# Causal mask of the row maxima: from a TensorE matmul to the VectorE instruction that takes the maximum

## The reference

```python
def attn(x, wq, wk, wv, wo):                  # x: 2 x 2048 x 1024, 32 heads of 32, one shared k and v
    q = (x @ wq).reshape(B, T, N_HEADS, HEAD_DIM)
    k = x @ wk
    v = x @ wv
    scores = jnp.einsum('bqhd,bkd->bhqk', q, k) * scale
    scores = jnp.where(causal[None, None], scores, -jnp.inf)
    probs = jax.nn.softmax(scores.astype(jnp.float32), axis=-1)
    out = jnp.einsum('bhqk,bkd->bqhd', probs, v).reshape(B, T, C)
    return out @ wo
def ffn(x, A, B, Wr, br):                     # 8 LoRA experts of rank 16, softmax router
    scores = H * jax.nn.softmax(jnp.einsum('bsd,hd->bsh', x, Wr) + br, axis=-1)
    low = jnp.einsum('bsd,hrd->bshr', x, A)
    return SCALING * jnp.einsum('bshr,hor,bsh->bso', low, B, scores)
x = x + layernorm(attn(layernorm(x)))
x = x + layernorm(ffn(layernorm(x)))
```

## Time and profile before

| what | value |
|---|---|
| time, 3 executions | median 3809.69 us (3802.37 to 3811.74) |
| the profiled execution: its own time | 3814.41 us |
| its span, first to last instruction | 3812.6 us |
| granted TensorE clock, mean | 0.953 of full speed |
| busy: PE, VectorE, ScalarE, GpSimd | 3486.0, 2466.2, 1574.0, 1927.6 us |
| diagonal head slots, mask matmuls L981 | 1024, 1024 |

### The profile page before, as it was taken

How to read it: one execution, slowest core, us unless ns; L and a number is a source line. 1 busy time by engine, 2 the same in 40 slices (tenths; PEclk the granted TensorE clock), 3 DMA queues, 4 the chain that set the end, 5 groups by cost and what they waited for, 6 DMA issues and landing times.

```text
span 3812.6 us, 47714 instructions
## 1 busy us (share of the span) xinstructions
PE 3486.0 (91%) x17496; PEld 1691.6 (44%) x17496; DVE 2466.2 (65%) x5584; ACT 1574.0 (41%) x3089; POOL 1927.6 (51%) x510
## 2 busy tenths in 40 slices
PE   5889999999999999899988999999999999999984
PEld 3444444444444444444444444444444444444432
DVE  3556776766767677874366667676777766667434
ACT  0223344444455444445322334344444554445541
POOL 0224455645455756566521355566355656566750
PEclk8989998999999999999998899999999999999995
DMA  3312111111011000001111211111100110000000
GB/s 79 121 42 76 33 38 34 56 34 37 20 34 56 20 26 26 20 20 29 62 51 38 71 34 45 32 40 51 39 26 26 29 30 24 26 20 15 18 1 33
DMA packets 132330, 144.19 MB, mean 38 GB/s; under 512 B 28024, under 2 KB 93560, under 8 KB 132096
## 3 DMA queue, kind: packets, MB, share of 16 engines
q1 hardware_dynamic: 132096, 141.13, 12.6%
HBM read 72.91 MB, written 16.78 MB: 24 GB/s over the span
## 4 chain that ended last, share of the span: by engine, by line
PE 69%; DVE 14%; POOL 7%; ACT 4%; issue 3%; SPq 2%; DMA 1%; POOLq 0%; ACTq 0%; DVEq 0%
PE ps L992 12%; PE ps L964 11%; PE ps L1007 11%; PE ps L978 11%; PE ps L1103 9%; POOL ds L514 5%; DVE mx L720 4%; DVE xr L818 2%; PE ps L1144 2%; PE ps L1016 2%; PE ps L1059 2%; SPq L415 2%; POOL ds L511 2%; PE ps L1038 2%; PE ps L1132 1%
## 5 line engine op out<-in xcount | busy, mean ns | idle before, releaser
L720 DVE TENSOR_REDUCE mx<-ps 128x1 f32<-128x512 f32 (+3 forms) x2560 | 1482.5, 601 | 939.2 <-PE ps L981 496.2
L555 ACT ACTIVATE pr<-ps 128x512 f32<-128x512 f32 (+3 forms) x2560 | 1321.8, 535 | 1651.5 <-PE ps L995 858.1
L514 POOL TENSOR_TENSOR ds<-ds,pr 128x2048 f32<-128x2048 f32 (+3 forms) x384 | 1565.2, 4076 | 572.3 <-ACT pr L555 546.2
L992 PE MATMUL ps<-qs,ks 98*128 98x512 f32 (+3 forms) x2560 | 1399.7, 550 | 53.8 <-ACT pr L555 38.6
L978 PE MATMUL ps<-ks,qs 96*128 96x512 f32 (+3 forms) x2560 | 1020.6, 408 | 83.8 <-DVE mx L720 60.7
L992 PEld LDWEIGHTS ps<-qs,ks 98*128 98x128 f32 x2560 | 499.6, 195 | 680.0 <-ACT pr L555 389.5
L511 POOL TENSOR_TENSOR ds<-pr 128x2048 f32<-128x2048 f32 (+1 forms) x64 | 273.3, 4271 | 880.5 <-ACT pr L555 880.5
L1007 PE MATMUL ps<-pr,vs 128*32 128x512 f32 (+3 forms) x5120 | 618.3, 555 | 0.0
L978 PEld LDWEIGHTS ps<-ks,qs 96*128 96x128 f32 x2560 | 510.8, 201 | 226.9 <-DVE mx L720 119.7
L964 PE MATMUL ps<-xT,wq_sb 128*128 128x512 f32 x1024 | 527.9, 616 | 7.3 <-DVE ks L786 4.2
L1103 PE MATMUL ps<-wo_sb,ao 128*128 128x512 f32 x928 | 489.1, 626 | 6.9 <-DVE q L715 2.8
(11 more groups left out here) (123 smaller groups left out, 2011.4 us busy)
## 6 DMA issues: line engine op xcount, KB each, us to landing
qs<-q SPq DMA_DIRECT2D x768, 64.0 KB, 2.0
wq_sb<-in_L_attn_wq_dram SPq DMA_DIRECT2D x64, 512.0 KB, 3.9
t<-in_L_attn_x_dram SPq DMA_DIRECT2D x32, 512.0 KB, 6.4
xr<-in_L_attn_x_dram SPq DMA_DIRECT2D x32, 512.0 KB, 3.5
out_dram<-xr SPq DMA_DIRECT2D x32, 512.0 KB, 2.6
qs<-mT SPq DMA_DIRECT2D x256, 4.0 KB
wo_sb<-in_L_attn_wo_dram SPq DMA_DIRECT2D x1, 4096.0 KB, 13.6
zs<-in_L_ffn_A_dram SPq DMA_DIRECT2D x1, 512.0 KB
```

Source lines behind the costliest of these rows:

```text
L514: nc.gpsimd.tensor_tensor(ds[:, :, c0:], ds[:, :, c0:], this, ALU.add).then_inc(added, 1)
L555: nc.scalar.activation(pr[:, k % NS, g, c0:], ps[:, PST + head(n, t, g) % NPS, c0:], ACT.Exp, scale=SCALE).then_inc(exp_done, 1)
L720: nc.vector.tensor_reduce(mx[:, qt * GH + g, c_:c_ + 1], ps[:, PM + head(n, s, g) % NPM, 0:w], AX.X, ALU.max).then_inc(mx_done, 1)
L992: last = nc.tensor.matmul(ps[:, bank, c0:], ks[0:STK + 2, c:c + P], qs[0:STK + 2, n % NS, g, c0:], start=True, stop=not diagonal)
```

## The change

In `max_scores` the mask matmul L981 is left out. In `maximum` a diagonal head slot is no longer reduced by `tensor_reduce` but by `tensor_tensor_reduce`, which adds `mask_qk` to the bank, writes the sum back to the bank and takes the maximum of it. `mask_qk` becomes 512 columns wide: 384 columns of zeros and then the 128 of the mask, so that its last `w` columns fit a slot of width `w`. In `scores` the mask matmul stays, with `mask_qk` as weights and the identity as the moving operand; `mask_kq` is dropped. The constants that nothing reads (`eps_sb`, `scratch`) are dropped too, and three [128, 1] buffers of the router share one.

```diff
-        mask_qk = sb("mask_qk", [P, P], BF16)
-        mask_kq = sb("mask_kq", [P, P], BF16)
+        mask_qk = sb("mask_qk", [P, BLK], BF16)
...
-        POOL_CONST = 10
+        POOL_CONST = 7
...
-            step(nc.gpsimd.affine_select(out=mask_qk[:, :], in_=mask_qk[:, :], compare_op=ALU.is_ge, fill=NEG,
+            step(nc.gpsimd.affine_select(out=mask_qk[:, BLK - P:], in_=mask_qk[:, BLK - P:], compare_op=ALU.is_ge, fill=NEG,
                                          base=0, pattern=[[-1, P]], channel_multiplier=1))
-            step(nc.gpsimd.memset(mask_kq[:, :], 0.0))
-            step(nc.gpsimd.affine_select(out=mask_kq[:, :], in_=mask_kq[:, :], compare_op=ALU.is_ge, fill=NEG,
-                                         base=0, pattern=[[1, P]], channel_multiplier=-1))
             step(nc.gpsimd.memset(ones[:, :], 1.0))
-            step(nc.gpsimd.memset(eps_sb[:, :], EPS))
...
             def maximum(n, s, g):
-                c_, qt, w, _ = item(n, s)
+                c_, qt, w, diagonal = item(n, s)
+                k = head(n, s, g)
+                seen, found = ps[:, PM + k % NPM, 0:w], mx[:, qt * GH + g, c_:c_ + 1]
                 dve.wait_ge(mx_ready, head(n, s, g) + 1)
-                nc.vector.tensor_reduce(mx[:, qt * GH + g, c_:c_ + 1], ps[:, PM + head(n, s, g) % NPM, 0:w], AX.X,
-                                        ALU.max).then_inc(mx_done, 1)
+                if diagonal:
+                    nc.vector.tensor_tensor_reduce(out=seen, in0=seen, in1=mask_qk[:, BLK - w:], op0=ALU.add, op1=ALU.max,
+                                                   scale=1.0, scalar=3.0 * NEG, accum_out=found).then_inc(mx_done, 1)
+                else:
+                    nc.vector.tensor_reduce(found, seen, AX.X, ALU.max).then_inc(mx_done, 1)
...
-                last = nc.tensor.matmul(ps[:, bank, 0:w], qs[0:STK, n % NS, g, qt * P:(qt + 1) * P],
-                                        ks[0:STK, c:c + w], start=True, stop=not diagonal)
-                if diagonal:
-                    last = nc.tensor.matmul(ps[:, bank, w - P:w], identb[:, :], mask_qk[:, :], start=False, stop=True)
-                last.then_inc(mx_ready, 1)
+                nc.tensor.matmul(ps[:, bank, 0:w], qs[0:STK, n % NS, g, qt * P:(qt + 1) * P],
+                                 ks[0:STK, c:c + w], start=True, stop=True).then_inc(mx_ready, 1)
...
-                    last = nc.tensor.matmul(ps[:, bank, c0:c0 + P], identb[:, :], mask_kq[:, :], start=False, stop=True)
+                    last = nc.tensor.matmul(ps[:, bank, c0:c0 + P], mask_qk[:, BLK - P:], identb[:, :], start=False, stop=True)
```

More of the change, by code:

```diff
@@ L233, in bass_mqa_sandwich_lora_router @@
         identb = sb("identb", [P, P], BF16)
-        mask_qk = sb("mask_qk", [P, P], BF16)
-        mask_kq = sb("mask_kq", [P, P], BF16)
+        mask_qk = sb("mask_qk", [P, BLK], BF16)
         ones = sb("ones", [P, HD])
-        eps_sb = sb("eps_sb", [P, 1])
         xr = sb("xr", [P, 2, D])
@@ L256, in bass_mqa_sandwich_lora_router @@
         ao = sb("ao", [P, NAO, BLK])
-        scratch = sb("scratch", [P, 4])
         m1 = sb("m1", [P, TB])
@@ L261, in bass_mqa_sandwich_lora_router @@
         lg = sb("lg", [P, NF])
-        nlm = sb("nlm", [P, 1])
         le = sb("le", [P, NF])
-        ls = sb("ls", [P, 1])
-        lr = sb("lr", [P, 1])
+        sm = sb("sm", [P, 3])
+        nlm, ls, lr = (sm[:, i:i + 1] for i in range(3))
         lw = sb("lw", [P, NF])
@@ L968, in max_scores @@
             def max_scores(n, s, g):
-                c, qt, w, diagonal = item(n, s)
+                c, qt, w, _ = item(n, s)
                 k = head(n, s, g)
```

## The result

| | before | with the change |
|---|---|---|
| median, 7 executions each | 3809.69 us | 3784.56 us (3774.95 to 3794.28) |
| ratio to before, 95% interval | | 0.9937 (0.9922 to 0.9952) |
| the same, measured again later (g0 below), 11 and 6 executions | 3814.56 us | 3781.52 us; 0.9918 (0.9904 to 0.9933) |
| mean granted clock of the profiled execution | 0.953 | 0.948 |

The account below looks back on a forecast made before the run. PE was taken to set the pace for two thirds of the time (69% of the chain). 54 - 18 + 0.5 = 36.5 us less, 3809.7 - 36.5 = 3773 us; range of 8 in 10 from 3730 to 3815.

Parts of the forecast that it names:

- TensorE gives back 54 us: First term: dropping the mask matmuls in the first pass saves TensorE 54 us, 49 + 12 - 7.
- The bounds of 30 and 87: TensorE's saving: 30 us if followers gain nothing and narrow slots half, 87 if all 1024 masks counted at 0.085.
- 165 narrow slots: Slots of 128 columns where the weight load partly fills the mask's place: 0.04 us off each, 7 us.
- VectorE's slots cost 18 us: Second term: diagonal slots take VectorE 0.156 us more each; 18 us are lost over 18 tight stretches.
- takes a full 0.144 us: VectorE's second instruction, writing one column of `mx`, waits for the first and costs 0.144 us; ends 0.06 and 0.18.
- The rule for idle time: Half of VectorE's idle time in a stretch hides its added 2.5 us; only the rest is lost.
- Small edits, 0.5 us: Fewer constants steps on GpSimd at the start save 0.5 us; exchanged mask operands and shared router buffers give nothing.
- VectorE takes it all back: Rival: VectorE's diagonal slots cost 0.25 us more each, 57 us in all; no change, about 3810 us; chance 0.13.
- Half speed: Rival: VectorE's new instruction needs a second cycle per column, 0.50 us a slot with the read; about 3940 us; chance 0.12.
- Every mask counts, 87 us: Rival: all 1024 masks on TensorE count at 0.085 us, VectorE hidden; 3723 us; chance 0.10.
- The busy column, 242.6 us: Rival: the mask matmuls' whole busy time on TensorE, 242.6 us, is saved; 3567 us; chance 0.03.
- the wide pairs: Sign: on TensorE, matmul pairs L975, L986 in wide diagonal slots start 0.48 us apart instead of 0.60.

Follow-up runs that it names:

- g0: The changed kernel unchanged, measured again beside the kernel before: 3781.5 us, 0.9918 of before.
- f0: The changed kernel with TensorE's mask matmul and VectorE's plain reduction back, so only the small edits are left: 3815.0 us, 1.0008 of before.
- e1: The changed kernel with no mask in the maxima, plain reduction on VectorE, second pass still masked: 3774.5 us, 0.990 of before.
- h0: The same kernel as e1, measured again: 3785.9 us, 0.9923 of before.
- e2: The changed kernel with TensorE's mask matmul put back, so both engines add the mask: 3833.4 us, 1.0043 of before.
- e3: The changed kernel, but in query block 0 (all-diagonal blocks) TensorE adds the mask and VectorE reduces plainly: 3785.6 us, 0.992 of before.
- g1: The changed kernel without its new VectorE instructions; TensorE's mask in query block 0 only, no mask in other blocks' maxima: 3783.1 us, 0.9927 of before.
- f1: The changed kernel, but in query block 0 TensorE adds a matmul of zeros where the mask stood: 3797.7 us, 0.996 of before.
- e4: The changed kernel, but VectorE adds the mask only in query block 0 and TensorE in the other blocks: 3823.3 us, 1.0018 of before.
- f2: The changed kernel with plain reductions everywhere; TensorE's mask in all blocks but query block 0, no mask in the maxima there: 3821.1 us, 1.0023 of before.
- f3: The kernel of e1 with 16 matmuls of zeros before TensorE's wait for the router's softmax: 3783.8 us, 0.9925 of before.
- g2: The kernel of g1 with two more matmuls of zeros behind each mask in query block 0: 3787.5 us, 0.9932 of before.

## Why the prediction was right in sign and too large

**TensorE gives back 54 us.** Mis-sized by a seventh: at an equal clock 46 to 47 us (3822 less 3775.4), which is 0.045 us for each of the 1024 masks; against f0 it is 49 us. The reading of start times was right for the pair; of the 0.12 us that a pair gives locally, somewhat over a third counts in the end. The bounds of 30 and 87 held, but the lower one was not worked out: 49 us with half of the 0.07 us of 165 narrow slots taken off is 43 (37 if 256 columns count as narrow too), not 30.

**VectorE's slots cost 18 us.** Too large: 3 to 5 us by e1, h0 and the changed kernel, 6 by e2 against f0 (7 to 8 against before). The step that failed is the sentence that the read, since it needs what the first instruction leaves, takes a full 0.144 us. The next main instruction starts beside it. The Trainium skill's rule to minimize the count of chained operations ("VectorE: DVE Perf Modes", Rules for kernel authors), which I had let decide for the upper value, did not hold for this pair at that price: the trace shows about 0.02 us more from slot to slot at 512 columns. The rule for idle time was too harsh in the six blocks, where e3 and g1 show no cost, to about 2 us; what there is stands in the all-diagonal blocks (4.4 us by f1 against e3, 2.4 by e4 against f2).

**Small edits, 0.5 us.** No gain is seen: f0's ratio shows no difference, and at an equal clock f0 is 2.5 us slower than before.

**What was missing: the clock.** No term stood for it. Before, the mean clock was 0.953 to 0.954, with the change 0.9476 and 0.9492: 0.004 to 0.006 less, 10 to 15 us. The sum is then -46.5 + 4 + 12.5 = -30 us, beside the measured 24 and 31; it has to come out near them, since the terms are taken from the same executions. The masks' matmuls were short but they were work on PE, in blocks where it stands idle for 50 of 486 us; the chain counted them only as cost. Without VectorE's new instructions the clock followed PE's work: lower with fewer matmuls (f2, e1, h0), higher with more (f3, g2). With them it was lower again (f1 against e3, e2 against before), and there more matmuls didn't raise it.

**Luck.** That the forecast came within 12 and 5 us is in part luck: 14 us too much for VectorE stood where 12 us for the clock were missing.

**The rivals.** VectorE takes it all back: no, it costs about a tenth of what PE gave back. Half speed: no, 700 ns at 512 columns. Every mask counts, 87 us: no. The busy column, 242.6 us: far off. Of the signs that the prediction named, L981 is gone and the wide pairs are 0.48 us apart as said; VectorE's busy time grew by 46 and not by 120 to 180 us.

**What stays open.** Why f1 and e2 lose clock isn't known. That PE waits longer for `mx_done` would be the obvious reason, but in the all-diagonal blocks these waits grew by 0.4 us only. Which block the clock's fall belongs to rests on one profile for each kernel, and a single profile's stretches scatter: the changed kernel's two have 0.887 and 0.913. A version that beats the changed kernel clearly was not found: e1 is 3 to 5 us faster at an equal clock, by the ratios (0.990 and 0.9923 against 0.9937 and 0.9918) this can't be told apart. It also needs 1024 VectorE instructions fewer.

## What to carry to other kernels

Read what a small matmul costs from the starts around it: here 0.12 us for the pair where its duration said 0.24, and 0.045 on average over the whole kernel. When matmuls are taken away in stretches where TensorE idles between them anyway, put a term for the granted clock into the sum; here it took back a quarter to a third of the gain, and in two blocks all of it (f2, e4). And when the clock of each execution is listed, compare kernels at an equal clock before explaining 10 us: two runs of one kernel whose medians differed by 11 us came out the same to within their errors of 1 us. Then hold the control (f0) to the same measure.

## What was not expected of the hardware

A `tensor_tensor_reduce` with its inputs in PSUM and SBUF bf16 runs at 700 ns for 512 columns and 291 for 128, and the read of its accumulator (141 ns) lies beside the start of the next one, so that the pair costs 0.62 to 0.64 us from start to start where a plain reduction takes 0.60 to 0.62.

The mean granted clock of a kernel on one core, whose TensorE is busy 90% of the time, differed from execution to execution between 0.949 and 0.957 for the same kernel, and with it the time by 27 us (3801.48 to 3828.47). At an equal clock 2.0 us of scatter is left.

That clock answered to VectorE's instructions as well: with TensorE's work unchanged and 256 `tensor_tensor_reduce` in place of plain reductions the mean clock was 0.9467 and not 0.9498 (f1, e3), with TensorE's waits for the maxima in those blocks at 9.7 and 9.3 us.
